# A 13x13 depthwise convolution on TensorE: from six products a channel to five, one of them on 64 output partitions

## The reference, cut to what matters

```python
dilates = (1, 1, 2, 3, 4, 5)
branch_ws = (w_b0, w_b1, w_b2, w_b3, w_b4, w_b5)
out = bn_eval(dwconv(x, w_lk, 1), bn_gamma[0], bn_beta[0], bn_mean[0], bn_var[0])
for i, (w, r) in enumerate(zip(branch_ws, dilates)):
    j = i + 1
    out = out + bn_eval(dwconv(x, w, r), bn_gamma[j], bn_beta[j], bn_mean[j], bn_var[j])
```

## Time and profile before

| | |
|---|---|
| median of 3 runs | 3388.57 us (3385.88 to 3396.99) |
| the profiled execution's own time | 3389.24 us |
| its span | 3387.5 us |
| mean granted PE clock | 0.983 of full speed |
| 13x13 stage, first product to last | from 3016.15 us, 367.32 us long |
| busy in the whole span | PE 97%, DVE 77%, ACT 60%, POOL 40% |

### The profile page before, as it was taken

The page is one execution under the profiler, slowest core; times in us unless marked ns, Lnnn a source line. Parts: engine busy times, 40 slices in busy tenths (PEclk is TensorE's granted clock), DMA queues, the critical chain, the costliest instruction groups (busy, mean ns, idle before and its releaser), DMA issues. The chain is left out here.

```text
span 3387.5 us, 88476 instructions
## 1 busy us (share of the span) xinstructions
PE 3271.3 (97%) x31488; PEld 3201.6 (95%) x31488; DVE 2623.6 (77%) x6557; ACT 2015.8 (60%) x5417; POOL 1339.9 (40%) x2738
## 2 busy tenths in 40 slices
PE   8999999999799999999969979999999899999999
PEld 6999999999799999999969979989999899999999
DVE  6888888888477777767669989979999788875554
ACT  5778878888344444444437756668999555532222
POOL 5777777777333333333214300024444466630000
PEclk9999999999899999999989989999999999999999
DMA  2444444321144444444369966645555788877775
GB/s 73 130 152 152 156 153 152 122 59 38 27 134 142 133 148 127 137 131 137 115 181 297 284 195 198 198 123 163 170 164 165 222 233 234 236 229 225 228 229 170
DMA packets 473932, 555.81 MB, mean 164 GB/s; under 512 B 79446, under 2 KB 332828, under 8 KB 473500
## 3 DMA queue, kind: packets, MB, share of 16 engines
q1 hardware_dynamic: 445844, 530.67, 53.0%
q10 hardware_dynamic: 27656, 19.48, 1.8%
HBM read 404.55 MB, written 258.73 MB: 196 GB/s over the span
## 5 line engine op out<-in xcount | busy, mean ns | idle before, releaser
L1594 PE MATMUL PS<-dw_grid,dw_mats 128*128 128x196 f32 (+1 forms) x3840 | 627.2, 327 | 26.7 <-DVE dw_mats L1523 26.7
L1594 PEld LDWEIGHTS PS<-dw_grid,dw_mats 128*128 128x128 f32 x3840 | 626.4, 192 | 27.1 <-issue 27.1
L1404 PE MATMUL PS<-mlp_w,mlp_hid 128*128 128x192 f32 x2352 | 414.4, 326 | 0.9 <-ACT mlp_hid L904 0.9
L1519 DVE COPY dw_grid<-X 32x392 f32<-32x392 f32 (+1 forms) x480 | 290.3, 605 | 158.9 <-PE PS L1594 147.9
L1404 PEld LDWEIGHTS PS<-mlp_w,mlp_hid 128*128 128x128 f32 x2352 | 378.6, 190 | 1.2 <-ACT mlp_hid L904 1.2
L1949 PE MATMUL PS<-grn_gain,down_hi 128*128 128x384 f32 x1176 | 352.3, 361 | 10.5 <-POOL X_low L1902 10.5
L1239 POOL TENSOR_TENSOR X<-X,mlp_b 128x192 f32<-128x192 f32 x196 | 112.5, 594 | 542.0 <-DVE mlp_xn L853 536.1
L904 ACT ACTIVATE mlp_hid<-PS,mlp_b 128x256 f32<-128x256 f32 x588 | 246.6, 471 | 111.3 <-PE PS L895 111.2
L610 ACT ACTIVATE att_vbd<-PS,att_rs 64x96 f32<-64x96 f32 x784 | 263.9, 337 | 21.0 <-DVE att_rows L522 13.6
L1902 POOL TENSOR_TENSOR X_low<-X,down_hi 128x128 fp32r<-128x128 f32 x196 | 214.0, 1092 | 146.7 <-ACT down_hi L1912 146.7
L1561 ACT ACTIVATE dw_res<-PS,dw_brow 128x196 f32<-128x196 f32 x192 | 81.5, 424 | 296.8 <-PE PS L1594 296.8
(11 more groups left out here) (283 smaller groups left out, 10197.8 us busy)
## 6 DMA issues: line engine op xcount, KB each, us to landing
scratch_hid<-hid_hid SPq DMA_DIRECT2D x196, 320.0 KB, 3.4
down_hid<-scratch_hid SPq DMA_DIRECT2D x196, 320.0 KB, 3.7
scratch_wide<-scratch_taps SPq DMA_DIRECT2D x64, 960.0 KB, 6.4
dw_raw<-scratch_wide SPq DMA_DIRECT2D x96, 640.0 KB, 4.4
scratch_wide<-scratch_taps SPq DMA_DIRECT2D x64, 768.0 KB, 4.8
dw_raw<-scratch_wide SPq DMA_DIRECT2D x96, 512.0 KB, 3.7
scratch_u<-mlp_u SPq DMA_DIRECT2D x56, 378.0 KB, 3.7
att_x<-in_x SPq DMA_DIRECT2D x196, 96.0 KB, 3.4
```

The source lines that it names most:

```text
L1404: last = nc.tensor.matmul(psD[i], hid[:, p.buf(2), m, i * 128:(i + 1) * 128], w2[:, m, :], start=(m == 0), stop=(m == MC - 1))
L1519: last = nc.vector.tensor_copy(dst, src)
L1594: last = nc.tensor.matmul(dst[:, :, ys, :], m, src, start=(i == 0), stop=(i == len(steps) - 1))
```

## The change

The output blocks of the last stage now begin two rows above the input's blocks. An output block then needs the rows of its own input block (y position 0), of the block above (-1) and, of the block below, only the upper part, since the 13 rows reach from -6 to +6 around an output row that lies two rows higher. There is one row of output blocks more, 15 instead of 14, and the host cuts the surplus rows off (`NOUT` = 2 x 15 x 7 = 210).

The products of a channel become: y position 0 with h = 0 over 15 block rows (210 columns), with h = 1 over 14 (196), y position -1 with h = 0 and h = 1 over 14 each (196), and, between these last two, one product for the blocks below: its moving operand `below` holds 32 partitions (the four upper rows) of each half for both x positions, 128 partitions in all, over 13 rows (182 columns), and its stationary operand `corner` is 128 x 64, since only the lower four rows of an output block are reached; it writes PSUM partitions 64 to 127.

Around it: the mats shrink from 24 to 16 rows, both halves are filled by copies of 128 x 512 elements, and no rows are cleared; the grid grows to 15 block rows and the clearing covers its first and last one; four copies of 32 partitions x 128 elements make `corner` on DVE; four copies of 32 partitions make `below`, the two of h = 0 on ACT ahead of its results, the two of h = 1 on POOL; PE waits for both before the product of the first channel of a pair; bias and output copies are 210 wide.

```diff
--- before.py
+++ after.py
@@ -37,6 +37,7 @@
 GR, GC = 13, 23
 NROWS = [16, 20]
 RUN = [rows * GP for rows in NROWS]
+NOUT = IMG * (BY + 1) * BX
 
 
 def first_row(i, line):
@@ -1444,22 +1445,45 @@
     U, HEAD, R, G = 8, 8, 4, 4
     CP = C // 2
     tall = turn == 1
-    rows = 24 if tall else 16
-    held = slice(2, 2 + NROWS[turn]) if tall else slice(0, rows)
+    rows = 16
+    top = NROWS[turn] - rows
     raw = s.sb("raw", [128, R, 2, RUN[turn]])
     mats = s.sb("mats", [128, R, 2, 2, rows, 16])
-    grid = s.sb("grid", [128, R, 2, IMG, BY + 1 - turn, BX + 1])
+    grid = s.sb("grid", [128, R, 2, IMG, BY + 1, BX + 1])
     brow = s.sb("brow", [128, C])
-    res = s.sb("res", [128, 2, G, NB]) if out is not None else None
+    wide_out = NOUT if tall else NB
+    res = s.sb("res", [128, 2, G, NOUT]) if tall else None
+    below = s.sb("below", [128, R, 2, IMG * BY, BX]) if tall else None
+    corner = s.sb("corner", [128, R, 2, top, 16]) if tall else None
+    below_act, below_pool = (s.sem("below_act"), s.sem("below_pool")) if tall else (None, None)
+    clears = 5 if tall else 2
     first = turn * CP
     stored = s.sems("stored", 2) if out is not None else None
     w1raw = s.sb("w1raw", [128, 2, HID]) if w1 else None
 
     def ps(b, c):
-        return PS[:, 2 * b.buf(4) + c, 0:NB]
+        return PS[:, 2 * b.buf(4) + c, 0:wide_out]
 
     def toeplitz(b, h):
-        return view(raw[:, b.buf(R), 0, 0:1], [[RUN[turn], 2], [GP, NROWS[turn]], [1, 16]], 16 * h)
+        return view(raw[:, b.buf(R), 0, 0:1], [[RUN[turn], 2], [GP, rows], [1, 16]], GP * top + 16 * h)
+
+    def corners(b):
+
+        for h in range(2):
+            for v in range(2):
+                taps = view(raw[64 * h:64 * h + 32, b.buf(R), 0, 0:1], [[RUN[turn], 2], [GP, top], [1, 16]], 16 * v)
+                yield corner[64 * h + 32 * v:64 * h + 32 * v + 32, b.buf(R), :, :, :], taps
+
+    def belows(t, b):
+
+        pair = bass.ds(t.n * 2, 2)
+        for h in range(2):
+            lines = X[64 * h:64 * h + 32, :, pair].rearrange("p (r x) c -> p c r x", x=BX)
+            for v in range(2):
+                first_x = h + v - 1
+                to = slice(max(0, first_x), BX + min(0, first_x))
+                yield (below[64 * h + 32 * v:64 * h + 32 * v + 32, b.buf(R), :, :, to],
+                       lines[:, :, :, to.start - first_x:to.stop - first_x])
 
     def copies(t, b):
 
@@ -1467,8 +1491,8 @@
         for h in range(2):
             if tall:
                 at_ = slice(64 * h, 64 * h + 64)
-                yield (grid[at_, b.buf(R), :, :, :, h:h + BX].rearrange("p c i y x -> p c (i y) x"),
-                       X[at_, :, pair].rearrange("p (r x) c -> p c r x", x=BX))
+                yield (grid[at_, b.buf(R), :, :, 0:BY, h:h + BX],
+                       X[at_, :, pair].rearrange("p (i y x) c -> p c i y x", i=IMG, y=BY))
             else:
                 for v in range(2):
                     at_ = slice(64 * h + 32 * v, 64 * h + 32 * v + 32)
@@ -1476,6 +1500,7 @@
                            X[at_, :, pair].rearrange("p (i y x) c -> p c i y x", i=IMG, y=BY))
 
     BY_ACT = 0 if tall else 1
+    BELOW_ACT = 2
 
     with nc.Block() as block:
         @block.sync
@@ -1498,17 +1523,26 @@
         def _(pool):
             lines = grid[:, :, :, :, :, :].rearrange("p r c i y x -> p (r c i y) x")
             nc.gpsimd.memset(lines[:, :, 0:BX + 1:BX], 0.0).then_inc(q["cleared"], 1)
-            if tall:
-                kernels = mats[:, :, :, :, :, :].rearrange("p r c h y x -> p (r c h) (y x)")
-                edges = view(kernels[:, 0, 0:1], [[rows * 16, 4 * R], [22 * 16, 2], [1, 32]])
-            else:
-                edges = view(grid[:, 0, 0, 0, 0, 0:1], [[(BY + 1) * (BX + 1), 2 * IMG * R], [BY * (BX + 1), 2], [1, BX + 1]])
-                pool.wait_ge(q["cleared"], 1)
+            edges = view(grid[:, 0, 0, 0, 0, 0:1], [[(BY + 1) * (BX + 1), 2 * IMG * R], [BY * (BX + 1), 2], [1, BX + 1]])
+            pool.wait_ge(q["cleared"], 2 * turn + 1)
             nc.gpsimd.memset(edges, 0.0).then_inc(q["cleared"], 1)
+            if not tall:
+                return
+            sides = below[:, :, :, :, :].rearrange("p r c l x -> p (r c l) x")[:, :, 0:BX:BX - 1]
+            nc.gpsimd.memset(sides, 0.0).then_inc(q["cleared"], 1)
+            pool.wait_ge(q["cleared"], clears)
+
+            def body(t):
+                b = t.ahead(first)
+                pool.wait_ge(q["conv"], b.n * 2 - 2 * R + 2)
+                for at_, src in list(belows(t, b))[BELOW_ACT:]:
+                    last = nc.gpsimd.tensor_copy(at_, src)
+                last.then_inc(below_pool, 1)
+            unrolled(CP, 0, body)
 
         @block.vector
         def _(dve):
-            dve.wait_ge(q["cleared"], 2 * turn + 2)
+            dve.wait_ge(q["cleared"], clears)
 
             def body(t):
                 b = t.ahead(first)
@@ -1520,7 +1554,10 @@
                 last.then_inc(q["grid_dve"], 1)
                 dve.wait_ge(loaded[b.buf(R)], b.turn(R) * 16 + 16)
                 for h in range(2):
-                    last = nc.vector.tensor_copy(mats[:, b.buf(R), :, h, held, :], toeplitz(b, h))
+                    last = nc.vector.tensor_copy(mats[:, b.buf(R), :, h, :, :], toeplitz(b, h))
+                if tall:
+                    for at_, taps in corners(b):
+                        last = nc.vector.tensor_copy(at_, taps)
                 last.then_inc(q["mats"], 1)
                 if w1 and t.n == 16:
                     w1.split(dve, w1raw)
@@ -1530,7 +1567,7 @@
 
         @block.scalar
         def _(act):
-            act.wait_ge(q["cleared"], 2 * turn + 2)
+            act.wait_ge(q["cleared"], clears)
 
             def body(t):
                 if t.inside(CP) and BY_ACT:
@@ -1541,6 +1578,12 @@
                     for dst, src in list(copies(t, b))[:BY_ACT]:
                         last = nc.scalar.activation(dst, src, ACT.Identity)
                     last.then_inc(q["grid_act"], 1)
+                if t.inside(CP) and tall:
+                    b = t.ahead(first)
+                    act.wait_ge(q["conv"], b.n * 2 - 2 * R + 2)
+                    for at_, src in list(belows(t, b))[:BELOW_ACT]:
+                        last = nc.scalar.activation(at_, src, ACT.Identity)
+                    last.then_inc(below_act, 1)
                 p = t.back(2)
                 if not p.inside(CP):
                     return
@@ -1583,12 +1626,19 @@
                 for c in range(2):
                     if b.reached(4):
                         pe.wait_ge(q["result"], b.n * 2 + c - 7)
-                    dst = ps(b, c).rearrange("p (i y x) -> p i y x", i=IMG, y=BY)
+                    dst = ps(b, c).rearrange("p (i y x) -> p i y x", i=IMG, x=BX)
                     if tall:
-                        steps = [(oy, h, 8 * (1 - oy), slice(max(0, -oy), BY - max(0, oy))) for oy in (0, -1, 1) for h in range(2)]
+                        steps = [(0, 0, 0, slice(0, BY + 1)), (0, 1, 0, slice(0, BY)), (-1, 0, 8, slice(1, BY + 1)), (-1, 1, 8, slice(1, BY + 1))]
                     else:
                         steps = [(1 - v, h, 8 * v, slice(0, BY)) for v in range(2) for h in range(2)]
                     for i, (oy, h, row, ys) in enumerate(steps):
+                        if tall and i == len(steps) - 1:
+                            if c == 0:
+                                pe.wait_ge(below_act, t.n + 1)
+                                pe.wait_ge(below_pool, t.n + 1)
+                            taps = corner[:, b.buf(R), c, :, :].rearrange("p r c -> p (r c)")
+                            src = below[:, b.buf(R), c, :, :].rearrange("p (i y) x -> p i y x", i=IMG)[:, :, 1:BY, :]
+                            nc.tensor.matmul(dst[128 - top * 16:128, :, 0:BY - 1, :], taps, src, start=False, stop=False)
                         m = mats[:, b.buf(R), c, h, row:row + 8, :].rearrange("p r c -> p (r c)")
                         src = grid[:, b.buf(R), c, :, ys.start + oy:ys.stop + oy, 1 - h:1 - h + BX]
                         last = nc.tensor.matmul(dst[:, :, ys, :], m, src, start=(i == 0), stop=(i == len(steps) - 1))
@@ -2015,8 +2065,8 @@
         v = np.ascontiguousarray(v)
         arrays["in_" + name] = v
         a[name] = nc.dram_tensor("in_" + name, v.shape, mybir.dt.from_np(v.dtype), kind="ExternalInput").ap()
-    out = nc.dram_tensor("out", [C, 128, NB], F32, kind="ExternalOutput").ap()
+    out = nc.dram_tensor("out", [C, 128, NOUT], F32, kind="ExternalOutput").ap()
     build(nc, a, out)
     r = run_bass_kernel_spmd(nc, [arrays], core_ids=[0])
-    y = r.results[0]["out"].reshape(C, 8, 16, IMG, BY, BX)
-    return np.ascontiguousarray(y.transpose(3, 0, 4, 1, 5, 2)).reshape(IMG, C, HW, HW)
+    y = r.results[0]["out"].reshape(C, 8, 16, IMG, BY + 1, BX)
+    return np.ascontiguousarray(y.transpose(3, 0, 4, 1, 5, 2).reshape(IMG, C, HW + 8, HW)[:, :, 2:HW + 2, :])
```

## The result

The changed kernel is slower: 3424.53 us median of five runs (3414.35 to 3430.20) against 3396.99 us of five runs of the kernel before (3385.88 to 3400.81). The ratio is 1.0081, 95% interval 1.0065 to 1.0097. The forecast was 3411.7 us in 3380 to 3430, slower with 0.77. It was made against one profiled execution of 3389.24 us; the profiled execution of the changed kernel took 3414.35 us, span 3412.5. So the two profiles lie 25.0 us apart, where the forecast had 22.5; the medians of five runs lie 27.5 apart.

The account below looks back on a forecast made before the run. PE alone was taken to set the end, bound by the columns streamed. Products -45.5, change of shape +67.2 and start +0.8 sum to +22.5 us, from 3389.2 to 3411.7 us, range 3380 to 3430.

Parts of the forecast that it names:

- The products: PE, last stage: five products a channel instead of six save 0.237 us, times 192 channels, -45.5 us.
- The slope of 0.84 ns a column: PE product records: 14 columns are worth 11.7 ns, giving 177.0 ns for 210 columns.
- The change of shape: PE around the 64-output corner: drains and bare weight loads cost 0.350 us a channel, +67.2 us.
- the two bounds: Shape price on PE: low 58.4 us from a transpose's load, high 100.2 us with whole mean load records bare.
- Rival C: PE at the corner: bare loads overlap their own product's columns, only drains of 37.2 us stay; 3381.7 us, 10%.
- Rival B: PE at the corner: changing shape has no price, as with alternating transposes; 3344.5 us, 10%.
- The start: Before the stage's first product: first mats copies of 0.89 us become 0.85 + 0.88, +0.8 us.
- Work beside PE: Copies per pair on DVE 2.94 us, ACT 2.45, POOL 2.3, all hidden under PE's 4.01 us.
- Rival D: POOL and DVE become the bound by waiting for each other: pair 5.2 us, 115 us on top, 3527; 8%.
- under 75%: Sign of a right forecast: DVE busy under 75% in the last stage, still waiting for PE.

Follow-up runs that it names:

- the run with the late POOL: Changed kernel with one more wait: POOL's first round of copies waits until the first pair's weights and corners are filled; 3413.35 us.
- the wide corner: Changed kernel with the corner matrix widened to 128 output columns, the first 64 zeros; 3394.46 us, beside 3392.41 for the kernel before.
- the fast version: Changed kernel with 128-column corner, its taps loaded by four transfers, one DVE corner copy, POOL's first round delayed; 3354.19 us median, ratio 0.9893.

## Why the prediction was right, and where it was off

**The products** (-45.5 us). The pair without any change of shape takes 3.317 us, before 3.793: 96 x 0.476 = 45.7 us less. The slope of 0.84 ns a column held within a nanosecond (0.177, 0.166, 0.154 us). The prediction's own record lengths are 0.5 ns short (157.5 ns as a mean, where the starts give 158.0 and a pair of 3.793), because the count of a window takes in records that its edges cut; this dropped out of the difference.

**The change of shape** (+67.2 us). Measured by itself in the kernel before, 65.7; taken out of the changed kernel, 65.6. The step was built from rows of other stages, one-column products and a product of 33 outputs; its parts came out as 0.093 and 0.092 for the drain beyond a usual step (taken: 0.097 less 0.002) and 0.053 and 0.104 for the bare loads (0.053 and 0.107). The measured price lies between the two bounds, 58.4 and 100.2. Two products side by side at one price show that it goes with the change.

**Rival C** (the loads overlap, 3381.7) has fallen: the loads are bare, in the record's length and in the steps between starts. **Rival B** (no price, 3344.5) has fallen at 64 outputs. A part of the case for it, the `128*96` transpose that "follows as smoothly", is what 96 outputs do in a real product as well: the reading of that row was sound for 96, and wrong only as a hint for 64. Why `128*64` transposes don't pay was not tried.

**The start** (+0.8 us) is the term that was mis-sized: +4.0. The step added 0.85 us of Toeplitz and 0.88 of corner copies at their undisturbed lengths, and took POOL as idle beside them. It isn't; it makes its rounds in advance there:

```profile
3014.04 7.65 POOL L1539 COPY dw_below<-X 32x392 f32<-32x392 f32 x8
3016.36 1.40 DVE L1557 COPY dw_mats<-dw_raw 128x512 f32<-128x512 f32 x2 [0.47 <-DMA dw_raw<-scratch_wide]
3017.68 3.31 DVE L1560 COPY dw_corner<-dw_raw 32x128 f32<-32x128 f32 x4
3021.09 2.34 PE L1644 MATMUL PS<-dw_grid,dw_mats 128*128 128x210 f32 x6 [10.09 <-DVE dw_corner L1560]
```

Four corner copies that take 0.90 us in the run with the late POOL take 3.31 here, each behind one of POOL's. Without POOL's copies the start is 5.83 us, with POOL later 5.67: +0.9 and +0.7 against 4.94, what the prediction had for it. The 0.9 us by which the stage began later and the 0.3 behind it were in no step.

**What of the hit was luck.** Between the profiles the forecast is 2.5 us short, because its errors partly cancel: products and shape came to 19.8 us instead of 21.7, the start to 3.2 more than forecast, and 1.2 lay outside the sum. Against the median of the runs, 3424.53, it is 12.8 us short; 7.8 of these come from the execution that it started from, which was that much faster than the kernel before is in the median of five runs (3396.99).

**Work beside PE.** DVE was put at 2.94 us a pair and "hidden", under 75%. Its own work is 2.75 us, but its busy time was 3.88, 97% instead of the "under 75%" that was to show it right: the Toeplitz copy takes 0.97 us beside POOL's, not 0.424. That costs nothing under PE's 4.000, as the run without POOL shows, so the sum was right by a cover and not by the number. POOL's two copies were put at 2.3 us; they take 1.72, and part of that is waiting for DVE, as shown below. Rival D (DVE and POOL as the bound) named the right mechanism and a fair limit: in its terms 2.94 + 2.3 exceeded 4.01. What it overrated is both POOL's time and the overlap that is lost: 2.75 us of DVE and 1.71 of POOL give 3.88, not 4.46. At 4.000 us it doesn't decide. It decides as soon as PE gets faster: 3.86 with two changes of shape, 3.84 with none. So removing the shape's price alone would not have given rival B's 3344.5; it gave 3394.5. It took POOL's copies away (3347), or fewer copies on DVE (3354), to come near.

The Trainium skill ("SBUF — State Buffer", "Who interferes with whom") has VectorE and GpSimd share a pair of ports; when a VectorE copy runs in one of its modes with two ports, whoever issues first holds the pair for the whole instruction and the other waits. No run here shows the mode, but the order of waiting agrees. Both engines in the changed kernel:

```profile
3200.26 0.85 POOL L1539 COPY dw_below<-X 32x392 f32<-32x392 f32 x1 [2.25 <-PE PS L1644]
3200.39 1.00 DVE L1557 COPY dw_mats<-dw_raw 128x512 f32<-128x512 f32 x1
3201.15 0.85 POOL L1539 COPY dw_below<-X 32x336 f32<-32x336 f32 x1
3201.32 0.97 DVE L1557 COPY dw_mats<-dw_raw 128x512 f32<-128x512 f32 x1
```

POOL's copies end at 3201.11 and 3202.01, DVE's at 3201.40 and 3202.29: 0.285 us behind POOL's each, and so it is, within 5 ns, for all 186 Toeplitz copies of the stage that began while one of POOL's ran. Where DVE began first it is the other way round; the run with both corners side by side:

```profile
3205.61 0.61 DVE L1553 COPY dw_grid<-X 64x392 f32<-64x392 f32 x1
3205.78 1.17 POOL L1539 COPY dw_below<-X 32x392 f32<-32x392 f32 x1 [1.65 <-PE PS L1645]
3206.23 1.14 DVE L1553 COPY dw_grid<-X 64x392 f32<-64x392 f32 x1
```

The first grid copy began before POOL's and keeps its usual 0.61 us. POOL's takes 1.17 and ends 0.73 behind it; the second grid copy, begun while POOL's ran, ends 0.42 behind POOL's. Which of the two waits is decided by which began first, and what the trace calls busy is partly waiting, on POOL too.

This fits with DVE standing at 97 and even 98.6% with a constant lead over PE: POOL's idle time is ended by PE, DVE's copies wait for POOL's, and so the share shows no slack. No run takes this chain apart. The bound shows elsewhere: in a lead of 0.1 us, and with the wide corner in PE's gaps.

## What to carry to other kernels

An f32 product of 64 outputs between products of 128 (33 paid a drain too) cost PE a third of a microsecond here for the way there and back, for one or two of them in a row; widened to 96 or 128 outputs it costs only its columns, and if it must stay narrow, put such products side by side. Before small copies go to an idle POOL, look at what DVE does at that moment and add the lengths, as the cautious bound, instead of hiding one under the other (2.75 and 1.71 us gave 3.88 here). A price for a stage that has never shown an operation can be put together from odd rows of other stages, if several widths lie on one line; the cover of hidden work has to be priced with its neighbours running.

## What the hardware showed that was not expected

- 96 outputs count as 128: no pause and no bare load (pair 3.317 us), while 64 outputs cost 0.342 us a channel on either half of the partitions. Widths between 64 and 96 were not tried.
- The drain was 0.093 us into the narrow shape and 0.092 out of it.
- Which copy waits, DVE's or POOL's, goes by which began first, and so which DVE copy pays depends on the phase: the Toeplitz copy (966 ns against 424) in the changed kernel, the grid copy (1090 against 604) with the wide corner, both (650 and 872), and POOL's own (1158), with the corners side by side.
- One DVE copy of 128 partitions and 128 elements, fed by four transfers, took 0.23 us alone at the start of the fast version, and 486 ns as a mean beside POOL; four of 32 partitions take 0.22 each.
